# Layer normalisation in front of expert, decay and attention stages: statistics in four groups of two tiles instead of three groups, the first low parts issued earlier, and the first gates' choice issued after the last low part

## The reference, cut to what matters

```python
x = x + attention(_layernorm(x), ...)       # 16 heads, causal
x = x + ffn(_layernorm(x), ...)             # 8 small experts, top 2 by gate
x = x + state_space(_layernorm(x), ...)     # 32 heads, segment sums
x = x + ffn(_layernorm(x), ...)             # the same experts again

def _layernorm(x, eps=1e-05):
    m = mean(x); v = var(x)
    return (x - m) / sqrt(v + eps)

# ffn: logits = x @ Wr + br + bonus; gates = softmax(logits); the two largest, renormalised,
#      weigh relu(x @ Wd + bd) @ Wu + bu
```

## Time and profile before

| | |
|---|---|
| median of 3 runs | 3033.44 us (3031.54 to 3035.66) |
| the profiled execution's own time | 3038.13 us |
| its span in the trace | 3036.2 us |
| PE busy | 2832.4 us, 93% of the span |
| DVE busy | 1945.2 us, 64% |
| ACT busy | 1203.6 us, 40% |
| POOL busy | 878.3 us, 29% |

### The profile page before, as it was taken

One profiled execution on the slowest core, in us unless ns is written; L12 is line 12 of the kernel. 1 busy time (PEld: TensorE's weight loads), 2 busy tenths in 40 slices (PEclk: granted clock), 3 DMA queues, 4 the chain that ended last, 5 costly groups with the idle time before them and its releaser, 6 DMA issues.

```text
span 3036.2 us, 59249 instructions
## 1 busy us (share of the span) xinstructions
PE 2832.4 (93%) x20484; PEld 2058.8 (68%) x20484; DVE 1945.2 (64%) x2948; ACT 1203.6 (40%) x1915; POOL 878.3 (29%) x1322
## 2 busy tenths in 40 slices
PE   3898999999998899999989989999999988999998
PEld 3655578777665568777765547877776555787776
DVE  2555566777745655777675547477776555757777
ACT  2244334444225434444323552444422454344442
POOL 3312212333222212333321231233333122123342
PEclk7999999999999999999999999999999999999999
DMA  9332111111233202111133220211123230211112
GB/s 350 94 70 66 34 46 41 49 50 49 85 80 67 50 22 56 44 51 47 42 99 77 50 50 22 65 51 47 40 71 92 50 81 19 58 48 47 45 46 81
DMA packets 163800, 192.20 MB, mean 63 GB/s; under 512 B 43962, under 2 KB 103994, under 8 KB 161786
## 3 DMA queue, kind: packets, MB, share of 16 engines
q1 hardware_dynamic: 155486, 175.31, 21.1%
q10 hardware_dynamic: 8096, 14.16, 1.5%
HBM read 106.99 MB, written 23.36 MB: 43 GB/s over the span
## 4 chain that ended last, share of the span: by engine, by line
PE 72%; DVE 15%; issue 5%; DMA 2%; ACT 2%; SPq 1%; POOL 1%; ACTq 1%; DVEq 0%; POOLq 0%
PE ps L768 16%; PE ps L769 15%; PE ps L770 15%; DVE mneg L1742 6%; PE ps L898 4%; PE ps L1163 4%; PE ps L955 3%; PE ps L937 2%; PE ps L1149 2%; PE ps L1172 2%; PE ps L893 2%; PE ps L1213 2%; DVE stats L1537 2%; DVE X L1593 1%; ACT PR L1363 1%
## 5 line engine op out<-in xcount | busy, mean ns | idle before, releaser
L768 PE MATMUL ps<-uh,win 128*128 128x512 f32 x1536 | 622.3, 405 | 0.6
L769 PE MATMUL ps<-ul,win 128*128 128x512 f32 x1536 | 601.1, 391 | 0.0
L770 PE MATMUL ps<-uh,win 128*128 128x512 f32 x1536 | 600.1, 391 | 0.0
L1742 DVE TENSOR_REDUCE mneg<-ps 128x1 f32<-128x128 f32 (+7 forms) x512 | 367.4, 753 | 346.9 <-PE ps L898 345.5
L1363 ACT ACTIVATE PR<-ps 128x1024 f32<-128x1024 f32 (+3 forms) x384 | 293.1, 807 | 309.9 <-PE ps L937 283.1
L2113 POOL TENSOR_SCALAR_AFFINE_SELECT LM<-LM 128x512 f32<-128x512 f32 x256 | 212.3, 840 | 501.4 <-ACT LM L1481 501.4
L768 PEld LDWEIGHTS ps<-uh,win 128*128 128x128 f32 x1536 | 288.5, 188 | 72.4 <-issue 9.5
L1856 DVE TENSOR_TENSOR LM<-ps,LM 128x512 f32<-128x512 f32 x256 | 170.3, 686 | 258.7 <-PE ps L1163 214.0
L770 PEld LDWEIGHTS ps<-uh,win 128*128 128x128 f32 x1536 | 288.4, 188 | 64.2
L769 PEld LDWEIGHTS ps<-ul,win 128*128 128x128 f32 x1536 | 289.1, 188 | 53.4
L955 PE MATMUL ps<-PR,V 128*32 128x512 f32 (+3 forms) x1536 | 286.6, 499 | 6.4 <-ACT OT L1373 3.8
(11 more groups left out here) (230 smaller groups left out, 5119.0 us busy)
## 6 DMA issues: line engine op xcount, KB each, us to landing
raw<-in_t SPq DMA_DIRECT2D x128, 256.0 KB, 2.8
QS<-EV SPq DMA_DIRECT2D x192, 128.0 KB, 2.6
KS<-EV SPq DMA_DIRECT2D x168, 128.0 KB, 2.6
in_t<-tiles ACTq DMA_DIRECT2D x10, 1024.0 KB, 9.5
XN<-in_L_attn_a_x_dram SPq DMA_DIRECT2D x40, 256.0 KB, 5.6
win_raw<-in_L_attn_a_Wqkv_dram SPq DMA_DIRECT2D x34, 256.0 KB, 3.4
win_raw<-in_t SPq DMA_DIRECT2D x32, 256.0 KB, 2.8
edec<-ed_t SPq DMA_DIRECT2D x512, 16.0 KB, 1.6
```

The costliest lines, as they stand in the source:

```text
L768: pe.matmul(dst, hi_l, hi_r, start=first, stop=False)
L769: pe.matmul(dst, hi_l, lo_r, start=False, stop=False)
L770: return pe.matmul(dst, lo_l, hi_r, start=False, stop=last)
L1742: dve.tensor_reduce(mneg[:, hh, t:t + 1], flat[:, off:off + (t + 1) * P], AX.X, ALU.max, negate=True).then_inc(a_max.sem, 1)
```

## The change

The statistics' groups become (0,1), (2,3), (4,5), (6,7), so that each normalisation has four aggregations and four inverse roots. `first_tiles` moves from behind the statistics of tile 3 to in front of the add of tile 4. `turned_tiles` moves from behind the statistics of tile 5 to behind those of tile 4, and at place B to behind those of tile 3. `center` of tile 3 moves in front of the last add's wait and the statistics of tile 7. `gate_choice(0)` moves from behind the logits of tile 5 to in front of the logits of tile 6, which puts it behind the low part of tile 7. At place B five of the eight fillers of 512 columns go. POOL's calls take the new count of groups.

```diff
-LN_GROUPS = [(0, 3), (3, 6), (6, 8)]
+LN_GROUPS = [(0, 2), (2, 4), (4, 6), (6, 8)]
...
                 w_add.wait(pe, b * 2 + 1, 3)
-                keep_awake(2, 8)
+                keep_awake(2, 3)
                 first_turns(b * 4 + 3)
...
             def by_tile(n, take, last_added, src):
 
+                center(n, 3, src)
                 last_added()
                 tile_stats(n, TT - 1, src)
-                center(n, 3, src)
                 for t in range(1, TT):
...
-            def add_tiles(n, product, added, bank, stats_of, src, loaded=None, banks=4):
+            def add_tiles(n, product, added, bank, stats_of, src, loaded=None, banks=4, lows_behind=HALF + 1):
 
                 for t in range(TT):
+                    if t == HALF:
+                        first_tiles(stats_of, src)
                     product.wait(dve, n, t + 1)
...
                         tile_stats(stats_of, t - 1, src)
-                        if t == HALF:
-                            first_tiles(stats_of, src)
-                        elif t == HALF + 2:
+                        if t == lows_behind:
                             turned_tiles(stats_of, src)
...
                 def behind(t):
+                    if t == HALF + 2:
+                        gate_choice(0)
                     logits(t)
...
-                    elif t == HALF + 1:
-                        gate_choice(0)
                     elif t == HALF + 2:
                         gate_weights(0)
...
-                add_tiles(b * 2 + 1, w_pe, w_add, 0, b * 4 + 3, X, banks=TT)
+                add_tiles(b * 2 + 1, w_pe, w_add, 0, b * 4 + 3, X, banks=TT, lows_behind=HALF)
...
-            inverse_roots(0, (0, 1))
+            inverse_roots(0, (0, 1, 2))
...
-                inverse_roots(b * 4, (2,))
+                inverse_roots(b * 4, (3,))
...
-                inverse_roots(b * 4 + 4, (0, 1))
+                inverse_roots(b * 4 + 4, (0, 1, 2))
```

## The result

The changed kernel took 3058.3 us (median of 5 runs, 3052.16 to 3065.18) against 3034.56 us for the kernel before (5 runs, 3031.54 to 3035.66). The ratio is 1.0074, with a 95% interval of 1.0060 to 1.0087: slower by about 22 us (the two medians are 23.7 apart). The forecast was 3056 us, range 3034 to 3065.

The account below looks back on a forecast made before the run. DVE's fixed work list was taken to set product 2, with PE the bound from there. Order, groups and gates' choice gave +2.6 us, the clock +20.1: +22.7 on 3033.44, so 3056 us, range 3034 to 3065.

Parts of the forecast that it names:

- DVE's list sets product 2: At B and C, DVE's fixed work list times the third low part; at B product 2 starts 0.36 us later.
- The extra group: In each normalisation, a fourth statistics group adds 0.45 us of DVE work.
- PE's pattern: At B, product 0's wait shrinks from 1.83 to 0.4 us; PE then stands 5 us behind product 1, but for one turn.
- Place A: One of four normalisation places: product 2 comes 0.62 us later; half of 1.7 us clock loss each, 3.4 together.
- Place B, the clock: At each B, a slow PE spell in front of product 2 is paid in full: 1.7 us, 6.8 together.
- Place C: At the normalisation place C: product 2 comes 0.24 us later; clock loss 1.2 us each, 4.8 together.
- The slow products 0 and 1 lie in time in which DVE was the bound: In the kernel before, slow-clock spells after the first low part's wait left the length of B the same.
- the walk: Step-by-step run through DVE's new order with traced durations; at C it put product 2 at +0.24 us.
- Place D: At the normalisation place D: turn 5 comes 0.65 us earlier; clock loss 1.7 us each, 5.1 together.
- The gates' choice: Moved behind the last low part, it brings the second gates 0.1 us earlier, eight times; PE waits for weights instead.
- The rival in which it would: Clock also falls at the experts, between product 7 and the weights: eight places at 1.3 us, 3066 us; chance 0.15.
- The rival *faster: Vanished slow spells at products 0 and 1, 8 x 1.7 us, are won: about 3020 us; chance 0.1.

Follow-up runs that it names:

- gap fillers: Changed kernel plus 30 unread 256-column products at place B, 16 ahead of turn 3 and 14 behind it: ratio 1.0033, 3050.39 us.
- the old order of low parts: Changed kernel with the first low parts behind the statistics of tile 5 again, at place B only: ratio 1.0029, 3046.14 us.
- the low parts back in the changed kernel: Changed kernel with the first low parts behind the statistics of tile 5 again at A, C, B and D: ratio 1.0010, 3039.94 us.
- With groups only: Kernel before with four groups of statistics and POOL's calls to match, nothing else: ratio 1.0011, 3039.74 us.
- the last two kernels: Kernel before with fillers at B and C and tile 7's statistics behind the third low part, 0.9966; the same plus the moved first gates' choice, 0.9962.
- the fastest version: Kernel before with fillers at B and C, tile 7's statistics later and the first gates' choice behind the last low part: 0.9962, 3024.08 us.
- the later tail alone: Kernel before with tile 7's statistics moved behind the third low part, without new fillers: ratio 1.0003, 3035.73 us.

## Why the prediction was right, point by point

The forecast of +22.7 us met +22.5 (0.0074 x 3034.56), and its mechanism is what the runs show: the stall moved from product 0 to behind product 1, the third low part came later, and the clock fell where PE is the bound. Its terms were less good than its sum. Measured in the profiled execution they add up to 16.8 us, not 22.7, and single executions of the changed kernel lie 13 us apart. That the sum met the medians to 0.2 us is luck.

- **DVE's list sets product 2: right.** The third low part at B comes 0.57 us later (predicted 0.47), product 2 0.54 later (0.36). Its start is 16.71 or 16.72 us behind the first add in the changed kernel, with gap fillers, and with the old order of low parts. The extra group is 0.42, predicted 0.45.
- **PE's pattern: right.** The wait in front of product 0 went from 1.83 to 0.56 us (0.4), product 1 ends near 791, and 5 us less one turn follow.
- **Place A: right in size, but not in its clock.** +0.57 was predicted as 0.62 less the gates' 0.1. The low parts waited 2.58 us for ACT's copy, as foreseen 2.7. The runs split it: -0.23 for the groups, +0.87 for the low parts' place, and -0.07 for the rest. Product 2 comes 19.34 us behind the first add instead of 18.70, +0.64 against +0.62 predicted. Its gap brought no fall of the clock in any of these kernels, so the 3.4 us put on it were 0.
- **Place B, the clock: right mechanism, mis-sized.** One spell of 1.7 us was the term. What came was twice that, 3.4 us of clock in each of four batches, and 2.2 to 2.7 of it reached the stretch: the rest of the spell lies in PE's own idle time. The term was 6.8 and measured 9.6.
- **Place C: too large.** 5.8 predicted, 3.3 measured. The clock fell in two batches of four, not in all. There it cost 1.2 to 1.3 us as predicted (31.83 and 31.67 against 30.50), but the falls before had not been free either: 0.9 us each (30.75 against 29.84). That price isn't the spell alone, for with the low parts back in the changed kernel the falls at the same place cost nothing; in the kernel before the fall comes with a centering of 1.63 us instead of 0.92 (first line below). "The slow products 0 and 1 lie in time in which DVE was the bound" holds at B to 0.03 us and not at C. Where the clock stayed up in both kernels C grew by 0.7 us, not by the walk's 0.24. Product 2 starts 16.27 us behind the first add (413.69 less 397.42) instead of 15.84, which is the group, and 0.2 more come behind it, from a step that the walk left out: center 5 runs beside POOL's subtraction. Timeline of the kernel before, first a batch whose clock fell at C and then one whose clock stayed up, and below it one of the kernel after whose clock stayed up:

```profile
412.14 1.63 DVE L1564 TENSOR_SCALAR xh<-X,mv,rstd 128x512 f32<-128x512 f32 x1 [0.25 <-PE ps L778]
...
1886.30 2.70 POOL L1989 TENSOR_TENSOR win<-win_raw,win 128x512 fp32r<-128x512 f32 x2
...
1886.94 0.92 DVE L1564 TENSOR_SCALAR xh<-X,mv,rstd 128x512 f32<-128x512 f32 x1
```
```profile
413.55 2.71 POOL L1989 TENSOR_TENSOR win<-win_raw,win 128x512 fp32r<-128x512 f32 x2
413.64 1.47 DVE L1564 TENSOR_SCALAR xh<-X,mv,rstd 128x512 f32<-128x512 f32 x1
```

  Its start fell 0.09 us behind POOL's instead of 0.64, and it took 0.55 us longer, as product 3 found.
- **Place D: the step that failed.** It said -0.65 us a batch for the order and +1.7 for the clock, and the stretch didn't change (42.9). Timeline of DVE at D, kernel before:

```profile
828.23 0.68 DVE L1712 TENSOR_TENSOR V<-ps,bvb 128x512 f32<-128x512 f32 x1
...
830.82 0.69 DVE L1712 TENSOR_TENSOR V<-ps,bvb 128x512 f32<-128x512 f32 x1 [0.85 <-PE ps L770]
...
831.88 0.69 DVE L1554 TENSOR_TENSOR ul<-ps,uh 128x512 fp32r<-128x512 f32 x1
```

  and kernel after, with PE's first value product and its turn 5:

```profile
826.76 0.50 PE L768 MATMUL ps<-wv,uh 128*128 128x512 f32 x1 [1.68 <-DVE ul L1554]
...
831.31 0.55 DVE L1564 TENSOR_SCALAR xh<-XN,mv,rstd 128x512 f32<-128x512 f32 x1 [1.84 <-issue]
...
833.07 0.69 DVE L1712 TENSOR_TENSOR V<-ps,bvb 128x512 f32<-128x512 f32 x1
...
834.74 0.68 DVE L1712 TENSOR_TENSOR V<-ps,bvb 128x512 f32<-128x512 f32 x1
...
835.78 0.69 DVE L1554 TENSOR_TENSOR ul<-ps,uh 128x512 fp32r<-128x512 f32 x1
...
836.62 0.63 PE L778 MATMUL ps<-ident,xh 128*128 128x128 f32 x4 [1.02 <-DVE ul L1554]
```

  D's first add is at 811.99 before and at 815.95 after. DVE's wait of 0.85 us for the value of tile 1 is gone, as foreseen. But its take of the value of tile 0 comes 17.12 us behind the first add instead of 16.24. So the low part of tile 3, for which turn 5 waits, comes at 19.83 instead of 19.89, and turn 5 at 20.67 instead of 20.72: -0.05 and not -0.65. The list had grown by what the wait gave back. Of the 0.88 us 0.42 are the extra group and 0.2 the idle time put down to "issue" at DVE's own loop's end (1.84 against 1.61); the rest was not split.

  The value product itself starts 10.81 us behind the first add instead of 10.95, though its low part ended 1.2 us earlier (9.47 against 10.70). With groups only, where that low part ends at 11.46, the product starts 0.14 us behind it. So in the changed kernel something else holds PE: it stands 1.1 to 2.0 us there in all profiles with the early low parts. The hardware loop's end lies there in PE's program. That the loop's turn is what holds PE fits, and no run tested it.

  The clock fell there in two of three batches and cost nothing in this execution (42.92 and 42.93 against 42.84 us). It wasn't free in others: the later spells of the kernel with gap fillers cost 1.7 and 2.6 us, the kernel with B's old order has one batch of 44.43, and in the last two kernels D took 41.81 and 41.90 us in the batch without a fall and 43.06 to 43.38 with one. So the kernel before most likely paid for its own three falls at D already, which the prediction took for free.
- **The gates' choice: right.** -0.05 to -0.1 us a stage was measured (A 37.33 against 37.38, and in the last two kernels B 33.02 against 33.15), and -0.1 forecast. The new wait of PE for the weights, kernel after:

```profile
806.01 0.39 PE L768 MATMUL ps<-wdr,uh 128*128 128x256 f32 x1 [0.34 <-DVE ul L1554]
...
810.30 0.33 PE L811 MATMUL ps<-ident,hg 128*128 128x128 f32 x1 [1.18 <-DVE hg L1650]
```

  Product 7's wait went from 1.00 to 0.34 us and came back as 1.18 in front of the weights' transpose. The list of waits shows 9.3 us of it, and no clock fell behind it. The rival in which it would did not come.
- **Not foreseen:** 1.1 us ahead of the first score maximum, in the part of the program that runs once. The same 324 matmuls keep PE busy there for 64.88 us instead of 62.70, at a mean clock of 0.77 instead of 0.78. The part ends at 115.7 to 117.4 us in the six profiles of kernels built on the kernel before, and at 116.9 to 119.5 in the seven of those built on the changed one. So some of it goes with the change, some is scatter, and its cause is open.

The rival *faster* ("the slow spells that disappear are worth their time if PE and not DVE sets product 2") was wrong for this change and turned out to be the lead to the fastest version. In the last two kernels the point "DVE's third low part comes before PE is ready" is passed, and there a held clock was worth 1.2 us at each B (33.15 against 34.37 in the kernel with the later tail alone).

## What to carry to other kernels

A stall can be moved for nothing, or for a loss: ask of each wait not how long it is but what runs behind it and who bounds that stretch, for a slow spell of PE was free under another engine's list and paid for the most part under PE's own. Two edits that do nothing alone (a shorter list on the bounding engine, fillers that hold the clock) can be worth 0.3% together, so test the pair before either is dropped. And a forecast whose sum is right should still be read term by term in the stretches: here the terms of B, A's clock and D were each off by 3 us or more, and partly cancelled.

## What the runs showed of the hardware that was not expected

- The clock fell in all four batches behind two idle times of 2.17 and 1.98 us with one turn of 0.66 us between, and for twice as long (3.4 us of clock lost) as behind one idle time of 1.8 us (1.7 us lost). A gap of 3.54 us with nothing in it, in the kernel with B's old order, lost only 1.7 us: the length of the gap is not what doubled it. Nor do the two idle times always double it: in the four kernels that have both idle times at B, 13 of 16 batches lost 3.4 us and three lost 1.7. What decides between the two is open. The Trainium skill ("TensorE: Matmul & The Clock Gate", section "A second HAM failure mode: psum-queue depth-cycling") tells of a kernel in which frequent short pauses between groups of products have the clock go down and up; the falls behind the two pauses here agree with that, and nothing here tests it for the doubling.
- Behind the same gap a fall is not certain: in the six kernels with the changed order at place C, 24 batches, the clock didn't fall in 6, lost 1.7 us in 15 and 3.4 us in 3. At A, where product 2 waits 1.34 us, it fell in none of the 24.
- At place C a centering beside POOL's subtraction takes 0.92 to 1.63 us instead of 0.54, and how much depends on where in it the centering starts: 1.47 when it starts 0.09 us behind, 0.92 at 0.64 us (the rows of place C above).
- POOL's inverse root is 0.85 to 0.88 us for three tiles. For two it is 0.69 to 0.72 us in 62 of the changed kernel's 67, but 0.82 to 0.99 us in all 16 of the kernel before, so a smaller group isn't always quicker. Why is open.
